# Feed-forward part of a Mamba layer: down projection three tiles behind, gate and up as one row, normalisation spread over engines

## The chip, the cores and the metric

The kernel runs on one core of a Trainium2 chip. Its time is device microseconds of one execution. The hardware profiler also records one execution of the kernel; all durations below are from it.

## The reference

x has 4 x 2048 tokens of 256 channels. Four Mamba layers run on the normalised x, their result is added to x, and a feed-forward part with FP4 rounding follows. Cut to what matters here:

```python
def fp4_quant_dequant(x):          # blocks of 16 along the last dimension
    scale = max(max(abs(block)) / 6.0, 1e-12)
    q = nearest of 0, 0.5, 1, 1.5, 2, 3, 4, 6 to abs(block / scale), with its sign
    return q * scale
def fp4_linear(x, w):
    return fp4_quant_dequant(x) @ fp4_quant_dequant(w).T
def ffn(x, w_gate, w_up, w_down):  # w_gate, w_up: 704 x 256; w_down: 256 x 704
    h = silu(fp4_linear(x, w_gate)) * fp4_linear(x, w_up)
    return fp4_linear(h, w_down)
x = x + mamba_layers(layernorm(x))
x = x + ffn(layernorm(x))
```

## The kernel before

Three parts follow each other, each a block with a program for every engine: `normalise_input`, `mamba_layers` and `fp4_ffn`. The first two are not touched. All data are fp32, and engines meet by semaphores alone: an engine executes its instructions in the order in which the program issues them, and a wait holds all that stands behind it on its engine. So the order within `turn`, written out by hand for each engine, sets everything.

`fp4_ffn` works on 16 chunks `g` of 512 tokens, each of four tiles `t` of 128 tokens (`tau = 4 * g + t` counts the 64 tiles). First the weights are rounded and turned (three pieces of gate and up, two of down). Then, per chunk: GpSimd adds x and the layers' result into `xa` (`add_x2`, L1398), VectorE takes statistics and mean and variance (L1448), ScalarE computes Ln and Exp for the root's first guess, with a table load for them and one more back to the Silu (L1319, L1367), VectorE refines and normalises into `xn` (L1458), and the chunk is rounded with `qa`. Per tile: TensorE turns the tile of `xq` (`turn_x`), ScalarE copies it to `xqT`, TensorE multiplies with the weights (`gate_up`, L1263) into `gate` and `up`, two PSUM banks each, ScalarE takes the Silu into `sg` (L1367), VectorE the product `hid` (L1508), which is rounded with `qh`; TensorE turns the rounded tile `hq` (`go_down`, L1239), ScalarE copies it to `hqT` (three copies, `copy_hT`), TensorE multiplies with `wdT` (`project_down`, L1280) into the one bank `down`, and VectorE adds `x2`, a copy of `xa` (L1363), and writes `res` (L1493), which SyncE stores.

A rounding (class `Fp4`) is a chain over three engines: VectorE takes the blocks' maximum, scale, nudged scale and reciprocal (`scales`, L1061 to L1068), GpSimd divides (L1073), VectorE masks the exponent (L1079), ScalarE turns it into a magic number with a Relu (`magic`, L1085), VectorE adds and takes it off (`shift` L1090, `unshift` L1095), GpSimd multiplies by the scale (L1101). `qh` has two buffers, `qa` one.

In `turn`, while tile `tau` is computed, the rounding of tile `tau - 1` is finished and the down projection of tile `tau - 2` is made; `before(g, t, n)` names the tile n back. The next chunk is added, normalised and rounded beside: statistics and normalisation at t = 0, divide at t = 1, multiply at t = 2. The chunk after that is loaded into `xa` and `xm` at t = 3, once `x2` is kept (t = 2).

## Time and profile before

| | us |
|---|---|
| median of 3 runs | 8876.52 |
| lowest, highest | 8876.08, 8879.55 |
| the profiled execution | 8879.16 |
| its span, first to last instruction | 8877.4 |
| feed-forward part, first gate matmul to the end | 1015.8 |

| engine | busy in the whole span, us |
|---|---|
| TensorE | 6565.6 |
| VectorE | 8002.6 |
| ScalarE | 5352.6 |
| GpSimd | 6905.2 |

The span is cut into 40 slices on the page; the first 35 are the Mamba layers with VectorE near full, the last five the feed-forward part with no engine over half or two thirds. Mean granted TensorE clock is 0.886 of full speed. A share of busy time is a mean over stages; the feed-forward part has to be read from its own timeline.

### The profile page before, as it was taken

To read this page: it belongs to the slowest core of one execution; us is meant where nothing else is said; L and a number is where in the kernel's file an instruction comes from. 1 tells how busy PE (TensorE), PEld (TensorE's weight loads), DVE (VectorE), ACT (ScalarE), POOL (GpSimd) and SP (SyncE) were. 2 spreads that over 40 slices of the span, in tenths; PEclk is the share of its full clock that TensorE was granted. 3 is DMA by queue.
4 is the path that set the end of the run, shared out by engine and by line. 5 is a ranking of instruction groups with operands and counts; after the bars stand their busy time and mean duration, and the time that the engine had idled before them with its cause. 6 is when DMAs were issued, how large, how long until landed. Compare 5 with 4: busy or idle time off the path is not lost. (4 is left out here: it accounts for less than half of the span.)

```text
span 8877.4 us, 97211 instructions
## 1 busy us (share of the span) xinstructions
PE 6565.6 (74%) x21284; PEld 2595.9 (29%) x21284; DVE 8002.6 (90%) x8268; ACT 5352.6 (60%) x8662; POOL 6905.2 (78%) x3198
## 2 busy tenths in 40 slices
PE   3777777778777777777777777777777777646656
PEld 1222222222222222222222222222222222224434
DVE  3999999999999999999999999999999999845555
ACT  2666666666666666666666666666666666422222
POOL 1888888888888888888888889888888889732222
PEclk9899998989899999898899989898989999767888
DMA  4444454544444544454445545444445455310000
GB/s 136 105 105 112 115 119 110 119 122 113 106 110 113 119 111 118 112 128 115 99 113 117 119 110 119 122 113 106 110 113 119 112 117 119 71 36 22 24 26 24
DMA packets 568694, 910.48 MB, mean 103 GB/s; under 512 B 58320, under 2 KB 203088, under 8 KB 566992
## 3 DMA queue, kind: packets, MB, share of 16 engines
q1 hardware_dynamic: 568016, 903.29, 42.4%
q8 instruction: 200, 3.28, 0.2%
q14 instruction: 478, 3.92, 0.2%
HBM read 716.41 MB, written 186.65 MB: 102 GB/s over the span
## 5 line engine op out<-in xcount | busy, mean ns | idle before, releaser
L832 POOL TENSOR_TENSOR hc<-h,crep 128x1024 f32<-128x1024 f32 x2048 | 4785.0, 2361 | 834.8 <-PE acc L473 748.6
L950 DVE TENSOR_TENSOR_SCAN h<-dA,carry,bu 128x512 f32<-128x512 f32 x3072 | 3768.2, 1265 | 92.7 <-ACT dA L603 46.7
L935 DVE TENSOR_TENSOR bu<-durep,B_all 128x1024 f32<-128x1024 f32 x2048 | 2483.2, 1212 | 194.6 <-DMA durep<-du_dram 146.1
L603 ACT ACTIVATE dA<-drep,cur 128x512 f32<-128x512 f32 x4096 | 2618.6, 710 | 14.5 <-DMA drep<-delta_dram 14.5
L455 PE MATMUL B_all<-dtc,spread_b 128*128 128x512 f32 x2048 | 1360.6, 752 | 1638.1 <-DVE bu L935 1636.6
L612 ACT COPY carry<-h 128x4 f32<-128x4 f32 x1023 | 200.9, 196 | 2223.5 <-DVE h L950 2168.7
L473 PE MATMUL acc<-hc,gather 128*32 128x512 f32 x8192 | 1281.8, 702 | 5.5 <-POOL hc L832 5.5
L950 DVE TENSOR_TENSOR_SCAN h<-dA,bu 128x512 f32<-128x512 f32 x1024 | 1196.7, 1206 | 9.9 <-ACT dA L603 7.8
L493 PE MATMUL work<-xT,inw 128*128 128x512 f32 x2048 | 1020.6, 644 | 60.5 <-ACT xT L623 50.0
L455 PEld LDWEIGHTS B_all<-dtc,spread_b 128*128 128x128 f32 x2048 | 367.6, 213 | 2321.5 <-DVE bu L935 2258.2
L503 PE MATMUL work<-xs,taps 128*128 128x512 f32 x2048 | 964.1, 614 | 0.0
L493 PEld LDWEIGHTS work<-xT,inw 128*128 128x128 f32 x2048 | 400.5, 207 | 758.9 <-issue 662.1
L1073 POOL TENSOR_TENSOR f_f_qh_xn<-f_hid,f_f_qh_rec 128x704 f32<-128x704 f32 x64 | 101.5, 1585 | 630.7 <-DVE f_f_qh_rec L1068 630.7
L503 PEld LDWEIGHTS work<-xs,taps 128*128 128x128 f32 x2048 | 376.1, 194 | 617.9 <-issue 617.9
L1280 PE MATMUL f_down<-f_wdT,f_hqT 128*128 128x256 f32 (+1 forms) x768 | 259.7, 494 | 341.1 <-ACT f_hqT L1329 341.1
L531 PE MATMUL work<-outw,sz 128*128 128x256 f32 x2048 | 489.6, 382 | 0.0
L473 PEld LDWEIGHTS acc<-hc,gather 128*32 128x32 f32 x8192 | 173.0, 116 | 979.8 <-issue 688.0
L844 POOL TENSOR_TENSOR quad<-quad,xs 128x2048 f32<-128x2048 f32 x64 | 289.4, 4522 | 160.2 <-ACT quad L701 160.2
L531 PEld LDWEIGHTS work<-outw,sz 128*128 128x128 f32 x2048 | 394.4, 193 | 55.6
L837 POOL TENSOR_TENSOR xc<-xc,quad 128x2048 f32<-128x2048 f32 x64 | 289.9, 4530 | 142.0 <-ACT quad L668 142.0
L462 PE MATMUL acc<-xc,skip 128*128 128x512 f32 x512 | 339.4, 752 | 0.0
L1280 PEld LDWEIGHTS f_down<-f_wdT,f_hqT 128*128 128x128 f32 (+1 forms) x768 | 177.4, 246 | 413.1 <-ACT f_hqT L1329 358.6
(167 smaller groups left out, 7151.8 us busy)
## 6 DMA issues: line engine op xcount, KB each, us to landing
drep<-delta_dram SPq DMA_DIRECT2D x1024, 256.0 KB, 6.0
durep<-du_dram SPq DMA_DIRECT2D x1024, 256.0 KB, 6.7
crep<-c_dram SPq DMA_DIRECT2D x1024, 64.0 KB, 6.5
delta_dram<-za SPq DMA_DIRECT2D x64, 1024.0 KB, 4.3
du_dram<-relu SPq DMA_DIRECT2D x64, 1024.0 KB, 5.3
x_in<-xbuf SPq DMA_DIRECT2D x65, 512.0 KB, 3.8
x_res<-xbuf SPq DMA_DIRECT2D x64, 512.0 KB, 3.9
xbuf<-x_res SPq DMA_DIRECT2D x64, 512.0 KB, 5.6
```

The costliest lines, as they stand in the source:

```text
L455: pe.matmul(B_all[:], spread_b[:, s % QS, :], dtc[:, p_, :], start=True, stop=True).then_inc(bb_ready, 1)
L462: pe.matmul(acc[:], skip[:, q, :], xc[:, p_, q, :], start=True, stop=False, skip_group_check=True)
L473: ins = pe.matmul(acc[32 * k:32 * k + 32, :], gather[:], hc[:, 4 * (s % 2) + k, :], start=False, stop=s % QS == QS - 1, skip_group_check=True)
L493: ins = pe.matmul(W[b][:], inw[:, k, z * DI + e * P:z * DI + (e + 1) * P], xT[:, k, :], start=k == 0, stop=k == KD - 1)
L503: ins = pe.matmul(W[b][:], taps[:, 4 * e + k, :], xs[:, e, k:k + T], start=k == 0, stop=k == 3)
L531: ins = pe.matmul(half, sz[:, p_, k, t * P:(t + 1) * P], outw[:, k, :], start=False, stop=k == DB - 1)
L603: act.activation(dA[:, 4 * (s % 2) + k, :], drep[q % 2][:, k, :], ACT.Exp, scale=cur[:, p_, 4 * s + k:4 * s + k + 1]).then_inc(da_ready, 1)
L832: pool.tensor_tensor(hc[:, pair, :], h[:, pair, :], crep[:, j:j + 1, :].to_broadcast([P, 2, T]), ALU.mult).then_inc(hc_ready, 1)
L837: pool.tensor_tensor(xc[:, p_], xc[:, p_], quad[:], ALU.mult).then_inc(xc_ready, 1)
L935: dve.tensor_tensor(bu[:, 2 * k:2 * k + 2, :], durep[q % 2][:, 2 * k:2 * k + 2, :], B_all[:].unsqueeze(1).to_broadcast([P, 2, T]), ALU.mul ...
L950: dve.tensor_tensor_scan(h[:, r, :], dA[:, r, :], bu[:, k, :], start, ALU.mult, ALU.add).then_inc(scanned, 1)
L1280: ins = pe.matmul(down[:, 0:D], hqT[0:rows, tt % 2, k, :], wdT[0:rows, k, :], start=k == 0, stop=k == GT - 1)
```

## The change

Only `fp4_ffn` and the layout of its weights change; the programs of the Mamba layers have the same instructions in the same order.

- Gate and up weights lie one behind the other without padding between them, and `gate_up` writes one row of 1,408 columns over three banks (`gu`), in pieces of 512, 512 and 384 columns; it waits until the last tile's `hid` is done. `down` has two banks.
- The down projection is three tiles behind, and its transposes stand ahead of the tile's gate/up, its matmuls behind. `hq` has four buffers.
- ScalarE copies `down` to `res` (`copy_res`, four tiles behind), and GpSimd adds `x2` to it (L1476). Two ScalarE copies of the turned tile instead of three.
- Mean and variance come from aggregate instructions on VectorE and small GpSimd operations; the Newton step is on GpSimd, the normalisation itself four ScalarE operations (L1327). Over the next chunk's four tiles: statistics, variance and root at t = 0; normalisation and scales at t = 1; divide, exponent, magic and first rounding at t = 2; second rounding and multiply at t = 3. The chunk after that is added at t = 3 and loaded at t = 1.
- On VectorE a tile's two roundings now stand ahead of the next tile's `hid`.

The diff, cut to its core:

```diff
-        gate, up = ps("gate", [P, 2, T]), ps("up", [P, 2, T])
...
+        gu = ps("gu", [P, 3 * T])
         hT = ps("hT", [P, 2, T])
         xTp = ps("xTp", [P, T])
-        down = ps("down", [P, T])
...
+        down = ps("down", [P, 2, T])
...
-                    at = before(g, t, 2)
-                    if at is not None:
...
-                    if t == 3 and not is_last(g):
+                    if t == 1 and not (isinstance(g, int) and g >= CH - 2):
                         sp.wait_ge(S["x2_kept"], g + 1)
-                        load((g + 2) % CH, par_)
+                        load(g + 2, par_)
+                    if at_least(g, 1):
+                        store(t, NT * g + t - NT)
...
-                for dst, at, sem_, free in ((gate, 0, S["gated"], None), (up, GT * P, S["up_done"], S["hid_ready"])):
...
-                    for half in range(2):
-                        for k in range(KD):
-                            ins = pe.matmul(dst[:, half, 0:HALF], xqT[:, t % 2, k, :],
-                                            wguT[:, k, at + half * HALF:at + (half + 1) * HALF],
-                                            start=k == 0, stop=k == KD - 1)
-                    ins.then_inc(sem_, 1)
+                    pe.wait_ge(S["hid_ready"], tau)
+                for at, width in SEGMENTS:
+                    for k in range(KD):
+                        ins = pe.matmul(gu[:, at:at + width], xqT[:, t % 2, k, :], wguT[:, k, at:at + width],
+                                        start=k == 0, stop=k == KD - 1)
+                    if at + width >= IN and at < IN:
+                        ins.then_inc(S["gated"], 1)
+                ins.then_inc(S["up_done"], 1)
...
                 pe.wait_ge(S["hT_copied"], tau + 1)
...
+                if positive(tau - 1):
+                    pe.wait_ge(S["res_copied"], tau - 1)
...
                     tau = NT * g + t
+                    at = before(g, t, 3)
+                    if at is not None:
+                        go_down(*at)
...
                     gate_up(tau, t)
                     if t < NT - 1:
                         turn_x(t + 1, tau + 1, g, par_)
-                    elif not is_last(g):
+                    if at is not None:
+                        project_down(*at)
+                    if t == NT - 1 and not is_last(g):
                         turn_x(0, tau + 1, g + 1, 1 - par_)
-                    at = before(g, t, 2)
-                    if at is not None:
-                        go_down(*at)
-                        project_down(*at)
...
+            def normalise(n, b):
+                act.wait_ge(S["root_done"], n + 1)
+                act.wait_ge(qa.xn_ready, GP + n)
+                for t in range(NT):
+                    ins = act.activation(xn[:, t], xa[:, b, t], ACT.Identity, bias=shift[:, t:t + 1],
+                                         scale=root[:, t:t + 1])
+                ins.then_inc(S["normed"], 1)
+            def keep_x2(g, b):
+                act.wait_ge(S["x2_ready"], g + 1)
...
+                act.copy(x2[:, b], xa[:, b]).then_inc(S["x2_kept"], 1)
...
+            def copy_res(tt, tau, chunk):
+                act.wait_ge(S["down_done"], tau + 1)
...
+                act.copy(res[:, tt], down[:, tt % 2, 0:D]).then_inc(S["res_copied"], 1)
...
-                    if t == 0 and not is_last(g):
-                        guess_root(g + 1)
-                    if t == 2:
-                        act.wait_ge(S["x2_ready"], g + 1)
...
-                        act.copy(x2[:], xa[:, par_]).then_inc(S["x2_kept"], 1)
+                    if at_least(g, 1):
+                        copy_res(t, tau - NT, g - 1)
+                    at = before(g, t, 3)
+                    if at is not None:
+                        hidden_turned(*at)
+                    at = before(g, t, 1)
+                    if at is not None:
+                        qh.magic(act, DP + at[1], at[0] % 2, minus_magic[:])
+                    if t == 0:
+                        keep_x2(g, par_)
+                    if t == 1 and not is_last(g):
+                        normalise(g + 1, 1 - par_)
                     act.wait_ge(S["gated"], tau + 1)
...
-                    act.activation(sg[:, t % 2].rearrange("p (a b) -> p a b", a=2), gate[:, :, 0:HALF],
-                                   ACT.Silu).then_inc(S["silu_done"], 1)
+                    act.activation(sg[:, t % 2], gu[:, 0:IN], ACT.Silu).then_inc(S["silu_done"], 1)
+                    if t == 0 and not is_last(g):
+                        guess_root(g + 1)
+                    if t == 2 and not is_last(g):
+                        qa.magic(act, GP + g + 1, 0, minus_magic[:])
                     if t < NT - 1 or not is_last(g):
                         copy_xT(t + 1, tau + 1)
-                    at = before(g, t, 1)
-                    if at is not None:
-                        qh.magic(act, DP + at[1], at[0] % 2, minus_magic[:])
...
+            def variance(n):
+                pool.wait_ge(S["means"], n + 1)
+                pool.tensor_tensor(ve[:], mv[:, :, 1], c_eps[:], ALU.add).then_inc(S["var_ready"], 1)
...
+            def newton_step(n):
+                pool.wait_ge(S["guess_ready"], n + 1)
+                pool.tensor_tensor(tmp[:], guess[:], guess[:], ALU.mult).then_inc(S["newton"], 1)
...
+                pool.tensor_tensor(shift[:], minus_mean[:], root[:], ALU.mult).then_inc(S["root_done"], 1)
...
             def turn(g, par_):
                 nxt, other = g + 1, 1 - par_
                 for t in range(NT):
                     tau = NT * g + t
+                    if at_least(g, 1):
+                        pool.wait_ge(S["res_copied"], tau - NT + 1)
+                        if t == 0:
+                            pool.wait_ge(S["x2_kept"], g)
+                        pool.tensor_tensor(res[:, t], res[:, t], x2[:, other, t], ALU.add).then_inc(S["res_ready"], 1)
+                    if not is_last(g):
+                        if t == 2:
+                            qa.divide(pool, GP + nxt, 0, flat_xn)
+                        if t == 3:
+                            quantise_x(nxt, other)
+                    at = before(g, t, 1)
+                    if at is not None:
+                        quantise_h(*at)
                     if t == 0 and not is_last(g):
-                        add_x2(nxt, other)
-                    at = before(g, t, 1)
+                        variance(nxt)
+                    if t == 3 and not (isinstance(g, int) and g >= CH - 2):
+                        add_x2(g + 2, par_)
                     qh.divide(pool, DP + tau, t % 2, hid[:, t % 2])
-                    if t == 1 and not is_last(g):
-                        qa.divide(pool, GP + nxt, 0, flat_xn)
-                    if t == 2 and not is_last(g):
-                        quantise_x(nxt, other)
-                    if at is not None:
...
-                        qh.multiply(pool, DP + at[1], at[0] % 2, hq[:, at[0] % 2])
+                    if t == 0 and not is_last(g):
+                        newton_step(nxt)
...
+            def scales_x(n):
+                dve.wait_ge(S["normed"], n + 1)
+                qa.scales(dve, GP + n, 0, flat_xn)
...
                     at = before(g, t, 1)
-                    if t == 0 and not is_last(g):
-                        normalise(nxt, other, 0)
                     if at is not None:
                         qh.exponent(dve, DP + at[1], at[0] % 2)
...
-                    dve.tensor_tensor(hid[:, t % 2].rearrange("p (a b) -> p a b", a=2),
...
+                    if not is_last(g):
+                        if t == 0:
+                            statistics(nxt, other)
+                        if t == 3:
+                            qa.unshift(dve, GP + nxt, 0)
                     if at is not None:
                         qh.shift(dve, DP + at[1], at[0] % 2)
+                        if t == 0 and not is_last(g):
+                            dve.wait_ge(S["stats"], nxt + 1)
                         qh.unshift(dve, DP + at[1], at[0] % 2)
+                    if not is_last(g):
+                        if t == 0:
+                            if at is None:
+                                dve.wait_ge(S["stats"], nxt + 1)
+                            moments()
+                        if t == 2:
+                            qa.exponent(dve, GP + nxt, 0)
+                    hidden(t, tau)
                     dve.wait_ge(S["hid_ready"], tau + 1)
                     qh.scales(dve, DP + tau, t % 2, hid[:, t % 2])
                     if not is_last(g):
-                        if t == 0:
-                            normalise(nxt, other, 1)
                         if t == 1:
-                            round_x(nxt)
+                            scales_x(nxt)
                         if t == 2:
                             qa.shift(dve, GP + nxt, 0)
-                            qa.unshift(dve, GP + nxt, 0)
-                    at = before(g, t, 2)
-                    if at is not None:
-                        add_residual(at[0], at[1], g if t >= 2 else g - 1)
```

How the instructions stand, in the loop that makes two chunks per iteration. GpSimd, before, one chunk from its first instruction (t = 0 to t = 3; `f_hq` is a tile's multiply, `f_f_qh_xn` its divide, `f_f_qa_xn` and `f_xq` the next chunk's divide and multiply):

```order
L1398 TENSOR_TENSOR f_xa<-f_xa,f_xm 128x1024 [waits f_in_loaded1]
L1073 TENSOR_TENSOR f_f_qh_xn<-f_hid,f_f_qh_rec 128x704 [waits f_qh_rec_ready]
L1101 TENSOR_TENSOR f_hq<-f_f_qh_q,f_f_qh_scale 128x704 [waits f_qh_rounded]
L1073 TENSOR_TENSOR f_f_qh_xn<-f_hid,f_f_qh_rec 128x704 [waits f_qh_rec_ready]
L1073 TENSOR_TENSOR f_f_qa_xn<-f_xn,f_f_qa_rec 128x1024 [waits f_qa_rec_ready]
L1101 TENSOR_TENSOR f_hq<-f_f_qh_q,f_f_qh_scale 128x704 [waits f_qh_rounded,f_hT_ready]
L1073 TENSOR_TENSOR f_f_qh_xn<-f_hid,f_f_qh_rec 128x704 [waits f_qh_rec_ready]
L1101 TENSOR_TENSOR f_xq<-f_f_qa_q,f_f_qa_scale 128x1024 [waits f_qa_rounded]
L1101 TENSOR_TENSOR f_hq<-f_f_qh_q,f_f_qh_scale 128x704 [waits f_qh_rounded,f_hT_ready]
L1073 TENSOR_TENSOR f_f_qh_xn<-f_hid,f_f_qh_rec 128x704 [waits f_qh_rec_ready]
```

The same chunk in the changed kernel, from the third divide on (t = 2 and t = 3):

```order
L1476 TENSOR_TENSOR f_res<-f_res,f_x 128x256 [waits f_res_copied]
L1073 TENSOR_TENSOR f_f_qa_xn<-f_xn,f_f_qa_rec 128x1024 [waits f_qa_rec_ready]
L1101 TENSOR_TENSOR f_hq<-f_f_qh_q,f_f_qh_scale 128x704 [waits f_qh_rounded,f_hT_ready]
L1073 TENSOR_TENSOR f_f_qh_xn<-f_hid,f_f_qh_rec 128x704 [waits f_qh_rec_ready]
L1476 TENSOR_TENSOR f_res<-f_res,f_x 128x256 [waits f_res_copied]
L1101 TENSOR_TENSOR f_xq<-f_f_qa_q,f_f_qa_scale 128x1024 [waits f_qa_rounded]
L1101 TENSOR_TENSOR f_hq<-f_f_qh_q,f_f_qh_scale 128x704 [waits f_qh_rounded,f_hT_ready]
L1417 TENSOR_TENSOR f_xa<-f_xa,f_xm 128x1024 [waits f_in_loaded0]
L1073 TENSOR_TENSOR f_f_qh_xn<-f_hid,f_f_qh_rec 128x704 [waits f_qh_rec_ready]
```

A tile's multiply stood behind its successor's divide and now stands ahead of it; the residual adds are new, and `f_xa` has moved from the chunk's start to behind the last multiply.

VectorE, before, from the product of t = 2 to that of t = 3:

```order
L1068 RECIPROCAL f_f_qh_rec<-f_f_qh_nudged 128x44 [waits f_qh_nudge_done]
L1090 SCALAR_TENSOR_TENSOR f_f_qa_q<-f_f_qa_ex,f_f_qa_xn 128x1024 [waits f_qa_magic_ready]
L1095 SCALAR_TENSOR_TENSOR f_f_qa_q<-f_f_qa_ex,f_f_qa_q 128x1024 [waits f_qa_shifted]
L1493 TENSOR_TENSOR f_res<-f_down,f_x 128x256 [waits f_res_stored0]
L1079 TENSOR_SCALAR f_f_qh_ex<-f_f_qh_xn 128x704 [waits f_qh_xn_ready]
L1508 TENSOR_TENSOR f_hid<-f_sg,f_up 128x704 [waits f_qh_xn_ready,f_up_done,f_silu_done]
L1090 SCALAR_TENSOR_TENSOR f_f_qh_q<-f_f_qh_ex,f_f_qh_xn 128x704 [waits f_qh_magic_ready]
L1095 SCALAR_TENSOR_TENSOR f_f_qh_q<-f_f_qh_ex,f_f_qh_q 128x704 [waits f_qh_shifted]
```

The changed kernel, at the same place:

```order
L1547 TENSOR_TENSOR f_hid<-f_sg,f_gu 128x704 [waits f_qh_xn_ready,f_up_done,f_silu_done]
L1061 TENSOR_REDUCE f_f_qh_amax<-f_hid 128x44 [waits f_qh_done,f_hid_ready]
L1064 TENSOR_SCALAR f_f_qh_scale<-f_f_qh_amax 128x44 [waits f_qh_maxed]
L1066 TENSOR_SCALAR f_f_qh_nudged<-f_f_qh_scale 128x44 [waits f_qh_scaled]
L1068 RECIPROCAL f_f_qh_rec<-f_f_qh_nudged 128x44 [waits f_qh_nudge_done]
L1090 SCALAR_TENSOR_TENSOR f_f_qa_q<-f_f_qa_ex,f_f_qa_xn 128x1024 [waits f_qa_magic_ready]
L1079 TENSOR_SCALAR f_f_qh_ex<-f_f_qh_xn 128x704 [waits f_qh_xn_ready]
L1095 SCALAR_TENSOR_TENSOR f_f_qa_q<-f_f_qa_ex,f_f_qa_q 128x1024 [waits f_qa_shifted]
L1090 SCALAR_TENSOR_TENSOR f_f_qh_q<-f_f_qh_ex,f_f_qh_xn 128x704 [waits f_qh_magic_ready]
L1095 SCALAR_TENSOR_TENSOR f_f_qh_q<-f_f_qh_ex,f_f_qh_q 128x704 [waits f_qh_shifted]
L1547 TENSOR_TENSOR f_hid<-f_sg,f_gu 128x704 [waits f_qh_xn_ready,f_up_done,f_silu_done]
```

The product `f_hid` stood ahead of the last tile's two roundings and is now behind them, the next chunk's first rounding stands at the end of t = 2 and the second between exponent and rounding of t = 3.

ScalarE, before, t = 0 (the chunk's first instructions):

```order
L1319 ACT_TABLE_LOAD
L1321 ACTIVATE f_lnv<-f_ve 128x4 [waits f_var_ready]
L1323 ACTIVATE f_guess<-f_lnv 128x4 [waits f_lnv_done]
L1367 ACT_TABLE_LOAD
L1367 ACTIVATE f_sg<-f_gate 128x704 [waits f_hid_ready]
L1349 COPY f_xqT<-f_xTp 128x256 [waits f_up_done,f_xT_ready]
L1085 ACTIVATE f_f_qh_ex<-f_f_qh_ex,f_minus_magic 128x704 [waits f_qh_ex_ready]
L1326 COPY f_hqT<-f_hT 128x512 [waits f_down_done]
L1328 COPY f_hqT<-f_hT 128x128
L1329 COPY f_hqT<-f_hT 64x128
```

The changed kernel, t = 0:

```order
L1357 COPY f_res<-f_down 128x256 [waits f_res_stored0]
L1338 COPY f_hqT<-f_hT 128x640 [waits f_down_done]
L1339 COPY f_hqT<-f_hT 64x128
L1085 ACTIVATE f_f_qh_ex<-f_f_qh_ex,f_minus_magic 128x704 [waits f_qh_ex_ready]
L1335 COPY f_x<-f_xa 128x1024 [waits f_res_ready]
L1393 ACTIVATE f_sg<-f_gu 128x704 [waits f_hid_ready]
L1316 ACT_TABLE_LOAD
L1318 ACTIVATE f_lnv<-f_ve 128x4 [waits f_var_ready]
L1320 ACTIVATE f_guess<-f_lnv 128x4 [waits f_lnv_done]
L1321 ACT_TABLE_LOAD
L1345 COPY f_xqT<-f_xTp 128x256 [waits f_up_done,f_xT_ready]
```

The two copies of the turned tile stood last and now stand near the front; Ln, Exp and the loads stood ahead of the Silu and are behind it, ahead of the copy to `f_xqT`.

## Rows read from the trace of the kernel before

**Rows 1.** Windows view: stretch, length, busy us of engines, granted clock, DMA share, GB/s.
```profile
8300.40:8365.24 64.84, 40.08 (x145) 26.57 (x144) 35.44 (x62) 15.96 (x30) 18.20 (x12) 0.82 0.07 24
...
7861.60:8877.40 1015.80, 643.14 (x2302) 425.91 (x2302) 557.16 (x966) 251.38 (x474) 282.73 (x173) 0.82 0.07 24
```

**Rows 2.** Timeline, one steady chunk: start, us, engine, line, out<-in [idle before <-releaser].
```profile
8300.40 2.63 PE L1263 MATMUL f_gate<-f_wguT,f_xqT 128*128 128x352 f32 x8
...
8306.85 2.34 POOL L1398 TENSOR_TENSOR f_xa<-f_xa,f_xm 128x1024 f32<-128x1024 f32 x1 [4.94 <-DMA f_xm<-xbuf]
...
8312.01 1.28 ACT L1367 ACT_TABLE_LOAD   x1
...
8337.77 5.65 PE L1280 MATMUL f_down<-f_wdT,f_hqT 128*128 128x256 f32 x12 [11.35 <-ACT f_hqT L1329]
...
8365.24 2.63 PE L1263 MATMUL f_gate<-f_wguT,f_xqT 128*128 128x352 f32 x8
```

**Rows 3.** Timeline, a tile of the last chunk.
```profile
8829.46 2.63 PE L1263 MATMUL f_gate<-f_wguT,f_xqT 128*128 128x352 f32 x8
...
8834.55 0.89 DVE L1508 TENSOR_TENSOR f_hid<-f_sg,f_up 128x704 f32<-128x704 f32 x1 [2.17 <-PE f_up L1263]
...
8836.70 3.05 PE L1280 MATMUL f_down<-f_wdT,f_hqT 128*128 128x256 f32 x12 [1.38 <-ACT f_hqT L1329]
...
8839.69 2.63 PE L1263 MATMUL f_gate<-f_wguT,f_xqT 128*128 128x352 f32 x8
```

**Rows 4.** Timeline, VectorE and GpSimd operations that meet.
```profile
8353.23 1.16 DVE L1090 SCALAR_TENSOR_TENSOR f_f_qa_q<-f_f_qa_ex,f_f_qa_xn 128x1024 f32<-128x1024 f32 x1
...
8353.39 2.24 POOL L1073 TENSOR_TENSOR f_f_qh_xn<-f_hid,f_f_qh_rec 128x704 f32<-128x704 f32 x1 [18.20 <-DVE f_f_qh_rec L1068]
...
8354.42 2.28 DVE L1095 SCALAR_TENSOR_TENSOR f_f_qa_q<-f_f_qa_ex,f_f_qa_q 128x1024 f32<-128x1024 f32 x1
...
8356.78 1.93 POOL L1101 TENSOR_TENSOR f_xq<-f_f_qa_q,f_f_qa_scale 128x1024 f32<-128x1024 f32 x1 [1.16 <-DVE f_f_qa_q L1095]
8356.96 2.14 DVE L1079 TENSOR_SCALAR f_f_qh_ex<-f_f_qh_xn 128x704 uint32<-128x704 uint32 x1
```

**Rows 5.** Timeline of the weights and the first chunk, where roundings run alone.
```profile
7836.02 1.38 POOL L1073 TENSOR_TENSOR f_f_qh_xn<-f_wd_in,f_f_qh_rec 128x704 f32<-128x704 f32 x1 [0.81 <-DVE f_f_qh_rec L1068]
...
7837.44 0.53 DVE L1079 TENSOR_SCALAR f_f_qh_ex<-f_f_qh_xn 128x704 uint32<-128x704 uint32 x1 [1.50 <-POOL f_f_qh_xn L1073]
...
7840.87 1.38 POOL L1101 TENSOR_TENSOR f_wdq<-f_f_qh_q,f_f_qh_scale 128x704 f32<-128x704 f32 x1 [3.47 <-DVE f_f_qh_q L1095]
...
7849.62 1.22 DVE L1061 TENSOR_REDUCE f_f_qa_amax<-f_xn 128x64 f32<-128x1024 f32 x1
...
7851.96 1.93 POOL L1073 TENSOR_TENSOR f_f_qa_xn<-f_xn,f_f_qa_rec 128x1024 f32<-128x1024 f32 x1 [7.40 <-DVE f_f_qa_rec L1068]
...
7868.51 0.89 DVE L1508 TENSOR_TENSOR f_hid<-f_sg,f_up 128x704 f32<-128x704 f32 x1 [3.54 <-PE f_up L1263]
...
7871.30 1.39 POOL L1073 TENSOR_TENSOR f_f_qh_xn<-f_hid,f_f_qh_rec 128x704 f32<-128x704 f32 x1 [8.67 <-DVE f_f_qh_rec L1068]
```

**Rows 6.** Timeline, the last Mamba layer's own normalisation.
```profile
7773.24 1.41 DVE L962 BATCH_NORM_STATS2 stats<-x_res 128x6 f32<-128x256 f32 x4 [21.33 <-ACT x_res L710]
...
7775.14 0.20 POOL L858 TENSOR_TENSOR ve<-mv,c_eps 128x4 f32<-128x4 f32 x1 [21.22 <-DVE mv L967]
...
7777.23 2.07 ACT L721 ACTIVATE x_res<-x_res,shift,root 128x256 f32<-128x256 f32 x4 [1.42 <-POOL shift L873]
```

**Rows 7.** Timeline of TensorE in a Mamba layer.
```profile
5037.42 3.70 PE L503 MATMUL work<-xs,taps 128*128 128x512 f32 x8
5044.41 1.12 PE L455 MATMUL B_all<-dtc,spread_b 128*128 128x512 f32 x2 [3.29 <-DVE bu L935]
...
5046.97 4.84 PE L503 MATMUL work<-xs,taps 128*128 128x512 f32 x8
```

**Rows 8.** Timeline, the last instruction on data.
```profile
8874.66 0.42 DVE L1493 TENSOR_TENSOR f_res<-f_down,f_x 128x256 f32<-128x256 f32 x1 [4.42 <-PE f_down L1280]
```

251 lines of the change are left out of this document (126 added, 125 removed).

## The prediction

> **What bounds the kernel now.** I read the 40 slices first: 35 of them are the four Mamba layers, which the change leaves alone, so only the feed-forward part counts. The windows view gives its length: from the first gate matmul to the end 1015.8 us [rows 1], for 16 chunks of four tiles. Then the timeline of one chunk: its first gate matmul starts at 8300.40 and the next chunk's at 8365.24, a period of 64.84 us, in which TensorE is busy 40.1, VectorE 35.4, GpSimd 18.2 and ScalarE 16.0 us [rows 1, 2]. No engine is full, so waits bound it. The timeline names them. GpSimd's `f_xa` add waits 4.94 us for a transfer issued only at the chunk's end; behind it stand statistics, Ln, a table load and the Silu, and behind that, on ScalarE, the copy of the turned hidden tile that `f_down` waits for. A tile later `f_down` waits 11.35 us for the same copy, which now stands behind the Relu of the next chunk's quantisation, and then takes 5.65 us, in part at the lower of the two clocks (granted 0.5, 1.2 of 2.4 GHz), against 3.05 [rows 2, 3]. In the last chunk, with no next one to prepare, tiles follow every 10.23 us (8829.46 to 8839.69), of which 1.38 is still `f_down` waiting for the copy [rows 3].
>
> **What the changed kernel can reach on TensorE.** Take that wait out: 10.23 - 1.38 = 8.85 us a tile. The gate/up row has the same 2,816 columns in pieces of 512 and 384, not 352. A matmul shows as two records. Eight records of 512 columns take 3.70 us and eight of 352 take 2.63 [rows 3, 7], the last one's tail of some 0.15 in both: 0.44 and 0.31 each, in proportion to their columns. The row costs the same 5 us, with 0.1 for what the tails leave unsure. A tile is then 9.0 us, a chunk 36: the floor. What removes the wait is that the hidden tile is turned before gate/up and its copy, about 1 us of ScalarE, is made during gate/up.
>
> **The rounding chain.** Per tile VectorE and GpSimd hand work to and fro, and the next product `f_hid` now stands behind the last tile's two roundings on VectorE. From rows without contention [rows 5]: product to start of the divide 7871.30 - 7868.51 = 2.79; divide 1.39; divide's end to start of the multiply 7840.87 - (7836.02 + 1.38) = 3.47, in which the exponent is 0.53 and the Relu and the two roundings are near 0.95 each with their handovers; I count 3.35 to the last rounding's end. Alone that is 2.79 + 1.39 + 3.35 = 7.5 us, under TensorE's 9.0. The question is what the chunk's extra work adds.
>
> **The shared port.** At 8353 the divide, 1.38 alone, takes 2.24: it starts 0.16 behind a VectorE rounding of 1.16 and ends 1.38 behind that one's end. The second rounding, of the same size, takes 2.28 and ends 1.07 behind the divide's end. At 8356.96 the exponent, 0.53 alone [rows 5], takes 2.14 and ends after the multiply that started 0.18 before it [rows 4]. So exponents, small scale operations and both roundings on VectorE never overlap a GpSimd tensor operation; who comes first holds the port to its end. After the change the port's work in a chunk is, on VectorE, 4 x (0.53 + 2 x 0.9 + 0.4 for two small ones) + 0.7 + 2 x 1.16 + 0.4 = 14.3 us (0.7: the chunk's exponent, scaled from 704 columns to 1,024), and on GpSimd 8 x 1.38 + 2 x 1.93 + 2.34 (the `f_xa` add) + eight small ones at 0.2 [rows 6] to 0.28 (1.8) + four residual adds: 21.5. No row shows a 256-column add: a quarter of the 1,024-column `f_xa` add is 0.59, and I take 0.6 (0.4, what VectorE needs for it, to 0.9). That is 35.8 us of a 36 us chunk: the port cannot be fully packed, so it and not TensorE decides.
> The Trainium skill ("Perfetto Trace Analysis", Optimizing Scalar/DVE Operations) says that moving work between GpSimd and VectorE may not help because they share a port. That speaks against the residual adds and the Newton steps on GpSimd; by it they are a part of the sum, as below.
>
> **One steady chunk, walked in order.** I count from the end of one tile's divide to the end of the next one's, with the program orders shown for the change. Where both engines want the port, the earlier one gets it; VectorE's next instruction starts some 0.1 us before GpSimd sees its semaphore.
> - Tile 0: residual add 0.6 (the exponent waits for it) + exponent 0.53 + statistics 1.4 (they cover the Relu; with the aggregate 1.9 [rows 6]) + roundings 1.85 + aggregate 0.4 + product to divide 2.7 + divide 1.39 = 8.9, less 0.2 where one instruction starts before the last one's end: 8.7.
> - Tile 1: five Newton operations 1.3 (they and the residual add let exponent and roundings through only in gaps); the normalisation, now four ScalarE operations, 2.07 by the same lines in the layer [rows 6], stands before the Silu, so the product starts 4.8 after the divide's end. + 2.8, then the scales of the next chunk, 2.34 by 7851.96 - 7849.62 [rows 5], which collide with the divide (1.4, beside them) and the add: +0.5. Until the chunk's scales are ready: 10.4.
> - Tile 2: exponent 0.45, the chunk's divide 1.93, and only then the roundings 1.85, the chunk's exponent 0.7, product to scales 2.7, the chunk's first rounding ahead of the divide 1.1, divide 1.38 = 10.1.
> - Tile 3: residual add 0.6, exponent 0.55, the chunk's second rounding 1.15, rounding 0.9, the chunk's multiply 1.93 (it was queued before the second rounding), rounding 0.9, product and maximum 1.7; then the `f_xa` add of 2.34, queued behind this tile's multiply, holds the port, +2.1 before the scales 0.85, divide 1.4 = 12.1.
> Sum 41.3 us; I take 41.2, since neighbours overlap by 0.1. TensorE needs 36 of it, so it idles 5.2. Most of that lies in one place: gate/up of tile 1 waits for the copy of its input, which stands on ScalarE behind Ln, Exp and a table load of 1.28 [rows 2], and these behind the variance, which GpSimd does after a multiply. `f_down` and the transposes before it are done 4.2 us earlier.
> **The clock.** Shortly after an idle stretch of 3.29 us the convolution's matmuls took 4.84 us, where they take 3.70 [rows 7]: 1.1 lost in this group alone; `f_down` after 11.35 us lost 2.6 [rows 2, 3]. I take 1.7, between them. The wait of 4.2 us is longer than the first, and the gate/up behind it has no slack there (its end starts the product), so all of it counts. A steady chunk is then **42.9 us**.
> **Off the path.** The longer residual path (ScalarE copy, GpSimd add, four tiles later), the `x2` copy (1.0, before a Silu with slack), one copy of 640 columns for two, stores and the loads, issued half a chunk earlier (the 4.94 us wait goes): 0. ScalarE has under 22 us of work. If the copies were late they would cost `f_down` up to 1.4 a tile, as now.
>
> **The whole.** Before the first gate/up: normalisation of chunk 0 by GpSimd and ScalarE instead of VectorE, about +1.1 (bounds 0 and 2). Chunk 0, without earlier tiles to finish, but with the cold clock: 37. Chunks 1 to 14: 14 x 42.9 = 600.6. Last chunk: its first gate/up starts 5.3 before the preceding divide ends; then 4 regular tiles to the last product, 28.4, and from there 0.9 + 1.9 + 1.4 + 3.35 + 1.4 + transposes 0.9, copy 1.0, `f_down` 3 to 5, copy and add 1.0, and 2.3 as now from the last residual's end (8875.08) to the end [rows 8]: 52.4 in all. Together 690 + 1.1 = 691 against 1015.8: **-324.7**. The span 8877.4 becomes 8552.7; the profiled execution took 8879.16, 1.8 more than its span, and 2.6 more than the median, so 8877 - 325 = **8552 us**.
>
> **Rivals.**
> - *The idle wait does not lower the clock*: chunk 41.2, 24 us less: 8528. For it: the fall shows some way behind the idle stretch, so part of it may find the engine waiting anyway.
> - *TensorE is the bound*, the port's collisions being hidden: chunk 36.5, 90 us less: 8463. For it: the last tiles of before run at 8.85 without the wait, though with VectorE at 6.1 of 10.2 [rows 1, 3]. Against: rows 4.
> - *GpSimd wins the ties*: the chunk's divide ahead of the exponent (+1.0), its multiply ahead of a rounding (+1.0), a tile's multiply ahead of the chunk's exponent (+0.7), and later variance (+0.4): chunk 46, 8596. The outer bound, VectorE's 31 and GpSimd's 21.5 never overlapping, is 52.5: 8688.
> - *Slower than before*: TensorE at its lower clock throughout. Every tile then costs 9.0 x 2 less its 0.4 of fixed parts = 17.6, a chunk 70.5, 5.6 more than now, x 14: 8955. It decides from 16.2 a tile, that is when over 80% of the time is at the lower clock. Against: a mean of 0.82 now [rows 1], with gaps of 10 us; mine are of 4.
> - *It does not do what it says*: the next chunk's input late again. The load is issued about 25 us ahead of its add, which waited 4.94: chance below 0.01.
>
> **Chances.** Forecast 0.51, no fall of the clock 0.15, TensorE bound 0.14, lost ties 0.17, TensorE at its lower clock 0.03, of which 0.01 lands within 0.2% of before because only most of the tiles are slow. Range 8465 to 8612: the forecast with residual adds of 0.4 to 0.9 (4 x 14 x 0.25 = 14 us), no fall, most of the third and of the fourth case. Faster by over 0.2% (18 us, about what a measurement of this kernel tells from no change): 0.97; within: 0.01; slower 0.02.
>
> **What would show it.** Right: chunks of 42 to 44 us; exponents in tile 2 or scales in tile 3 of 2 us behind GpSimd's operations; one idle stretch of TensorE of about 4 us before the second gate/up, for the copy of `f_xqT`, with the granted clock at 0.5 behind it. Wrong: uniform tiles of 9 us with TensorE near 100% (second rival), or TensorE waiting for `f_hid` in most tiles (more ties lost). If GpSimd's adds and VectorE's roundings are seen side by side at their own durations, the sum fails at the port.

## The result: 8522.8 us, 29 us below the forecast, and the profile after

| | before | after |
|---|---|---|
| median | 8876.3 us | 8522.8 us (8518.0 to 8525.1) |
| profiled execution and its span | 8879.16, 8877.4 | 8524.19, 8522.4 |
| a steady chunk | 64.84 | 40.97 |
| first gate matmul, start | 7861.6 | 7860.75 |

The ratio is 0.9604 (95% interval 0.9587 to 0.9621). All medians in this document are of executions in the chip's fast state; one of the four of e9 below took 8910.2 us at a lower clock and is left out. The Mamba layers are untouched; the feed-forward part went from 1015.8 us [rows 1] to 661.65. The windows view of the changed kernel, with the columns of rows 1 (a steady chunk, then the whole part):

```profile
8197.58:8238.55 40.97, 36.11 (x128) 21.34 (x128) 31.73 (x47) 19.43 (x35) 23.48 (x24) 0.96 0.12 38
7860.75:8522.40 661.65, 582.42 (x2046) 342.07 (x2046) 494.18 (x737) 304.75 (x534) 365.58 (x357) 0.95 0.11 35
```

TensorE is busy for 36.1 of 41.0 us, VectorE 31.7, GpSimd 23.5, and the mean granted clock rose from 0.82 to 0.96. The 4.94 us that GpSimd waited for the transfer and the 11.35 us that `f_down` waited for its copy [rows 2] have no counterpart in the steady chunk. One long wait of TensorE is left. The timeline of the second tile shows it (start, us, engine, line, out<-in, idle before and its releaser):

```profile
8193.83 1.39 POOL L1101 TENSOR_TENSOR f_hq<-f_f_qh_q,f_f_qh_scale 128x704 f32<-128x704 f32 x1 [3.56 <-DVE f_f_qh_q L1095]
...
8195.17 0.20 POOL L1421 TENSOR_TENSOR f_ve<-f_mv,f_c_eps 128x4 f32<-128x4 f32 x1
...
8195.41 0.20 ACT L1318 ACTIVATE f_lnv<-f_ve 128x4 f32<-128x4 f32 x1 [0.95 <-POOL f_ve L1421]
...
8195.87 1.28 ACT L1321 ACT_TABLE_LOAD   x1
...
8197.16 0.37 ACT L1345 COPY f_xqT<-f_xTp 128x256 f32<-128x256 f32 x1
...
8197.58 6.42 PE L1258 MATMUL f_gu<-f_wguT,f_xqT 128*128 128x512 f32 x12 [4.31 <-ACT f_xqT L1345]
...
8202.75 0.76 ACT L1393 ACTIVATE f_sg<-f_gu 128x704 f32<-128x704 f32 x1 [1.01 <-PE f_gu L1258]
...
8204.10 0.89 DVE L1547 TENSOR_TENSOR f_hid<-f_sg,f_gu 128x704 f32<-128x704 f32 x1 [2.20 <-PE f_gu L1258]
```

The chain is to be read downwards: GpSimd's multiply, behind it the variance, then Ln on ScalarE, the table load, the copy to `f_xqT`, and only then gate/up, after 4.31 us of idle. Gate/up takes 6.42 us, where the other tiles take 4.89 to 4.96, and the Silu and the product wait for it (2.20). The granted clock, microsecond by microsecond (the column behind the engines' busy times):

```profile
8196.00:8197.00 1.00, 0.00 (x0) 0.00 (x0) 0.60 (x2) 1.00 (x1) 0.28 (x1) 1.00 1.07 359
8197.00:8198.00 1.00, 0.41 (x1) 0.42 (x2) 0.00 (x0) 0.99 (x4) 1.00 (x1) 0.55 0.06 17
8198.00:8199.00 1.00, 1.00 (x2) 0.42 (x2) 0.53 (x1) 0.85 (x3) 0.84 (x4) 0.50 0.00 0
8199.00:8200.00 1.00, 1.00 (x2) 0.34 (x1) 0.39 (x1) 0.92 (x2) 0.85 (x3) 0.50 0.00 0
8200.00:8201.00 1.00, 1.00 (x3) 0.45 (x2) 0.97 (x1) 1.00 (x3) 0.23 (x1) 0.75 0.00 0
8201.00:8202.00 1.00, 1.00 (x4) 0.41 (x3) 0.89 (x1) 0.74 (x2) 0.00 (x0) 1.00 0.39 131
```

It stands at 0.50 (1.2 of 2.4 GHz) from 8198 to 8200 and is back at 1.00 from 8201 on: some 3 us at half speed, which is the 1.5 us that this gate/up takes more than the others. And the port that VectorE and GpSimd share, at five places of a chunk (the first in the chunk before):

```profile
8189.54 0.72 POOL L1476 TENSOR_TENSOR f_res<-f_res,f_x 128x256 f32<-128x256 f32 x1
8189.61 1.03 DVE L1079 TENSOR_SCALAR f_f_qh_ex<-f_f_qh_xn 128x704 uint32<-128x704 uint32 x1 [1.50 <-POOL f_f_qh_xn L1073]
...
8206.73 1.16 DVE L1061 TENSOR_REDUCE f_f_qa_amax<-f_xn 128x64 f32<-128x1024 f32 x1
8206.89 1.39 POOL L1073 TENSOR_TENSOR f_f_qh_xn<-f_hid,f_f_qh_rec 128x704 f32<-128x704 f32 x1 [3.46 <-DVE f_f_qh_rec L1068]
...
8208.24 0.72 POOL L1476 TENSOR_TENSOR f_res<-f_res,f_x 128x256 f32<-128x256 f32 x1
8208.36 0.65 DVE L1066 TENSOR_SCALAR f_f_qa_nudged<-f_f_qa_scale 128x64 f32<-128x64 f32 x1
...
8221.26 2.51 POOL L1101 TENSOR_TENSOR f_xq<-f_f_qa_q,f_f_qa_scale 128x1024 f32<-128x1024 f32 x1 [1.60 <-DVE f_f_qa_q L1095]
8222.02 2.50 DVE L1095 SCALAR_TENSOR_TENSOR f_f_qh_q<-f_f_qh_ex,f_f_qh_q 128x704 f32<-128x704 f32 x1
...
8226.01 2.35 POOL L1417 TENSOR_TENSOR f_xa<-f_xa,f_xm 128x1024 f32<-128x1024 f32 x1
8226.28 2.12 DVE L1064 TENSOR_SCALAR f_f_qh_scale<-f_f_qh_amax 128x44 f32<-128x44 f32 x1
```

The exponent (0.53 alone [rows 5]) takes 1.03 behind the residual add, a scale step of 64 columns 0.65 (0.20 in e11 below, where no add stands beside it), the rounding 2.50 behind `f_xq` (0.89 alone), a scale of 44 columns 2.12 behind the `f_xa` add. The pair at 8206.73 is the counterexample: a reduction and a divide side by side, each at its own duration. The Trainium skill ("SBUF — State Buffer", section "SBUF: two separate sides") has the pair of ports as an exclusive lock, which a VectorE operation needs in a two-port mode or with two SBUF inputs, and which whoever starts first holds for the whole instruction. The roundings, with two inputs in SBUF, were held, and the reduction, with one input, was not; that agrees. The exponent and the scale steps also have one input and were held, so by that sentence they must run in a two-port mode, which no view here shows.

### The profile page after: what moved, and what is told of

It is laid out like the page before. It is cut to its first block and busy times, and to the rows that moved or that the text cites. A ratio compares the mean times of both kernels' runs of the same rounds, so it can differ in the third digit from the quotient of the medians.

```text
span 8522.4 us, 96647 instructions
## 1 busy us (share of the span) xinstructions
PE 6497.0 (76%) x21028; PEld 2513.0 (29%) x21028; DVE 7936.9 (93%) x8028; ACT 5407.2 (63%) x8725; POOL 6990.0 (82%) x3390
## 5 line engine op out<-in xcount | busy, mean ns | idle before, releaser
L1258 PE MATMUL f_gu<-f_wguT,f_xqT 128*128 128x512 f32 (+1 forms) x768 | 341.7, 598 | 72.8 <-ACT f_xqT L1345 65.9
L854 POOL TENSOR_TENSOR relu<-za,xc 128x2048 f32<-128x2048 f32 x64 | 290.5, 4539 | 0.1
L850 POOL TENSOR_TENSOR za<-quad,relu 128x2048 f32<-128x2048 f32 x64 | 290.0, 4531 | 0.1
```

Of the source, the lines that this page charges most:

```text
L854: pool.tensor_tensor(relu[:], za[:], xc[:, p_], ALU.mult).then_inc(du_ready, 1)
L1258: ins = pe.matmul(gu[:, at:at + width], xqT[:, t % 2, k, :], wguT[:, k, at:at + width], start=k == 0, stop=k == KD - 1)
```

## Experiments

The experiments were run in three groups, each on a chip of its own beside the kernel before, whose median there was 8876.4 us (e1 to e4), 8872.3 (e6 to e9) and 8870.0 (e10, e11, b1, b3). So a difference of medians between two groups is uncertain by some 6 us, and the ratio or the chunk is the safer measure. A chunk's length is the distance of one gate/up from the same one of the next chunk.

| kernel | median us | ratio to before, 95% | chunk us |
|---|---|---|---|
| changed kernel | 8522.8 | 0.9587 to 0.9621 | 41.0 |
| e1 copy first | 8501.9 | 0.9563 to 0.9595 | 39.2 |
| e2 idle filled | 8532.1 | 0.9597 to 0.9629 | 41.0 |
| e3 add early | 8497.2 | 0.9556 to 0.9588 | 39.1 (mean) |
| e4 thin residual | 8519.0 | 0.9582 to 0.9614 | 41.0 |
| e8 = e4 and e1 | 8478.6 | 0.9537 to 0.9569 | 37.7 |
| e7 = e1 and e3 | 8487.5 | 0.9549 to 0.9581 | 38.7 |
| e9 turned behind | 8517.5 | 0.9584 to 0.9623 | 40.3 |
| e6 product first | 8633.2 | 0.9712 to 0.9745 | 47.8 |
| e10 = e6 and e1 | 8575.9 | 0.9651 to 0.9683 | 44.4 |
| e11 residual on VectorE, with e1 | 8470.8 | 0.9531 to 0.9563 | 37.8 |
| b1, before with Relu behind the copy | 8732.2 | 0.9827 to 0.9860 | 54.6 |
| b3 = b1 and load ahead | 8684.3 | 0.9774 to 0.9807 | 51.2 |

### The idle wait and the clock: e1, e2

e1 puts the copy to `f_xqT` ahead of Ln, Exp and the table load, on ScalarE:

```diff
                     act.activation(sg[:, t % 2], gu[:, 0:IN], ACT.Silu).then_inc(S["silu_done"], 1)
-                    if t == 0 and not is_last(g):
-                        guess_root(g + 1)
                     if t == 2 and not is_last(g):
                         qa.magic(act, GP + g + 1, 0, minus_magic[:])
                     if t < NT - 1 or not is_last(g):
                         copy_xT(t + 1, tau + 1)
+                    if t == 0 and not is_last(g):
+                        guess_root(g + 1)
```

> One move in the changed kernel: at t = 0 ScalarE copies the next tile's input to f_xqT ahead of Ln, Exp and their two table loads, not behind them. Theory (chain over VectorE and GpSimd through the shared port, plus a clock fall after the idle stretch): gate/up of t = 1 starts at the end of the last product, 2.7 us earlier, at full clock, and takes 4.9 instead of 6.4 us; the product of t = 1 is then held by the normalisation, the Silu and the roundings and comes 1.55 us earlier. Chunk 40.96 -> 39.4 us, time 8523 -> about 8500. If TensorE's work were the bound: the whole idle stretch of 4.3 us is won, chunk 36.7, about 8459. If GpSimd and VectorE alone set the period and the clock costs nothing: 8523 unchanged.

It measured 8501.9 us, as expected. The wait of 4.31 us is gone, and that gate/up takes 4.96 us. But the clock still falls in about every second chunk, at another gate/up, the one behind the Relu of the next chunk's rounding. Timeline of e1, two chunks in a row:

```profile
8204.82 6.62 PE L1258 MATMUL f_gu<-f_wguT,f_xqT 128*128 128x512 f32 x12 [1.58 <-ACT f_xqT L1345]
...
8244.00 4.99 PE L1258 MATMUL f_gu<-f_wguT,f_xqT 128*128 128x512 f32 x12 [1.49 <-ACT f_xqT L1345]
```

The chunks with and without this fall are 39.2 and 39.3 us long, so here the lower clock costs nothing: the next product does not wait for this group's end. e2 leaves the wait and fills it with matmuls whose results nobody uses:

```diff
                         go_down(*at)
+                    if t == 1 and at is not None:
+                        pe.wait_ge(S["res_copied"], tau - 4)
+                        for _ in range(14):
+                            pe.matmul(down[:, at[0] % 2, D:2 * D], ident[:], wdT[:, 0, :], start=True, stop=True)
                     gate_up(tau, t)
```

> Added in the changed kernel: at t = 1 TensorE executes 14 matmuls of 256 columns into an unused half bank, 3.5 us, in the stretch in which it waits for f_xqT; their results are not used. Nothing waits less. Theory of the clock fall: gate/up of t = 1 starts as before but takes 4.9 instead of 6.4 us, chunk 40.96 -> 39.5, about 8502. If the idle stretch had nothing to do with the long gate/up, or if TensorE were the bound: unchanged at 8523 or slower by up to what the filler overruns, 0.5 us a chunk, 8530.

It measured 8532.1 us, a miss. The timeline of TensorE and ScalarE in e2, then the window of its gate/up:

```profile
8194.74 6.21 PE L1302 MATMUL f_down<-f_wdT,f_ident 128*128 128x256 f32 x28
...
8198.78 0.37 ACT L1349 COPY f_xqT<-f_xTp 128x256 f32<-128x256 f32 x1
...
8200.78 4.89 PE L1258 MATMUL f_gu<-f_wguT,f_xqT 128*128 128x512 f32 x12
```

```profile
8200.78:8205.67 4.89, 4.89 (x15) 2.39 (x14) 2.26 (x2) 3.25 (x6) 2.38 (x4) 1.00 0.08 27
```

Gate/up takes 4.89 us at a granted clock of 1.00. So it is the idle stretch that brings the low clock to this group. But I had counted the 14 matmuls as 14 records, and a matmul is two: the filler took 6.21 us instead of 3.5 and ended 1.6 us after the copy (8198.78 + 0.37 to 8200.78). That is as much as the clock had cost (1.5), hence the same chunk of 41.0. The mechanism is shown, the gain of a better-sized filler is not.

### The port: e4, e8, e11

e4 cuts GpSimd's residual add to one column; its output lacks `x2` in the other 255.

```diff
-                        pool.tensor_tensor(res[:, t], res[:, t], x2[:, other, t], ALU.add).then_inc(S["res_ready"], 1)
+                        pool.tensor_tensor(res[:, t, 0:1], res[:, t, 0:1], x2[:, other, t, 0:1], ALU.add).then_inc(S["res_ready"], 1)
```

> The residual adds in GpSimd's loop are made for one of 256 columns (the output lacks x2 elsewhere): 0.72 us each becomes about 0.15. Shared port theory: the exponents of t = 0 and t = 3 (1.03 instead of 0.53), a rounding of t = 1 (1.36 instead of 0.89) and a small operation of t = 2 (0.65 instead of 0.19) no longer wait, about 1.8 us a chunk: 39.2, about 8497. Without a shared port: GpSimd has idle time ahead of each of its other operations, so nothing, 8523.

It measured 8519.0 us, no gain clear of the noise, though the port theory asked for 26 us. The timeline of e4 has both halves of the answer:

```profile
8188.63 7.89 PE L1258 MATMUL f_gu<-f_wguT,f_xqT 128*128 128x512 f32 x12 [3.58 <-ACT f_xqT L1345]
...
8190.65 0.89 DVE L1090 SCALAR_TENSOR_TENSOR f_f_qh_q<-f_f_qh_ex,f_f_qh_xn 128x704 f32<-128x704 f32 x1 [0.95 <-ACT f_f_qh_ex L1085]
...
8196.61 0.89 DVE L1547 TENSOR_TENSOR f_hid<-f_sg,f_gu 128x704 f32<-128x704 f32 x1 [4.14 <-PE f_gu L1258]
```

The rounding behind the add is back at its own 0.89 (1.36 in the changed kernel), so the port is relieved. But gate/up of the same tile now takes 7.89 instead of 6.42 us and the product waits 4.14 for it: this time the lower clock (0.63 in the mean over this group) covered more of it, 3.0 us more than 4.89 against 1.5, and it took the gain back. The wait ahead of it is shorter than in the changed kernel, 3.58 us against 4.31, so the deeper fall does not come from a longer idle stretch, as I wrote in the expectation of e8. e8 tests that reading by making the same cut with the copy first (the same part of the output is missing):

> The residual add cut to one column (the output lacks x2 in the other 255), together with the copy to f_xqT ahead of Ln and Exp. The thin add alone gave 8519, no gain, though the VectorE steps behind it went back to their own durations. My theory: the gain was eaten by the longer idle of TensorE and the deeper fall of its clock ahead of the second gate/up of a chunk; with the copy first that wait is gone, and the port time comes through: 8502 less 15 x 1.8 = 8475. Rival: the residual adds' port time was hidden all along: 8500.

It measured 8478.6 us, 23 us under e1 (1.5 a chunk), where 27 were expected and the rival had none. Its chunk:

```profile
8191.64:8229.36 37.72, 34.95 (x128) 20.76 (x128) 29.79 (x48) 18.85 (x35) 21.34 (x23) 1.00 0.13 42
```

A clock of 1.00 throughout and 37.7 us. The residual adds do cost what they hold of the port. GpSimd's own time is not what they cost: in e1 it waits 0.7 to 3.6 us behind each of the four adds for its next input. e11 turns that into a kernel with the whole output: VectorE adds `x2` straight from PSUM, in gaps in which it waits, and the ScalarE copy and the GpSimd add go.

```diff
+            def add_residual(t, tau, g_of, b):
+                dve.wait_ge(S["down_done"], tau + 1)
...
+                dve.tensor_tensor(res[:, t], down[:, t % 2, 0:D], x2[:, b, t], ALU.add).then_inc(S["res_ready"], 1)
...
                         qh.exponent(dve, DP + at[1], at[0] % 2)
+                    if t in (1, 2) and at_least(g, 1):
+                        add_residual(t, tau - NT, g - 1, other)
...
                             qa.shift(dve, GP + nxt, 0)
+                    if t in (0, 3) and at_least(g, 1):
+                        add_residual(t, tau - NT, g - 1, other)
```

> The changed kernel with the early copy to f_xqT, and with the residual add on VectorE straight from PSUM, as in before (0.42 there), in the gap in which VectorE waits for the Relu (t = 1, 2) or for the divide (t = 0, 3); no ScalarE copy to f_res, no GpSimd add. Port theory: the 0.72 us of GpSimd leave the port in every tile, and the 0.42 on VectorE fall into gaps: as with the one-column add, chunks of 37.8, 8479. Rival (VectorE's own time counts, and its read of x2 holds the port too): 39.3 + 4 x 0.4, 8520.

It measured 8470.8 us, 52 us under the changed kernel and the fastest kernel with the whole output (e8 lies within its interval). Timeline and window of e11:

```profile
8215.60 2.08 POOL L1073 TENSOR_TENSOR f_f_qa_xn<-f_xn,f_f_qa_rec 128x1024 f32<-128x1024 f32 x1 [0.94 <-DVE f_f_qa_rec L1068]
8215.82 0.41 DVE L1522 TENSOR_TENSOR f_res<-f_down,f_x 128x256 f32<-128x256 f32 x1
```

```profile
8221.46:8259.27 37.81, 35.17 (x129) 20.72 (x129) 31.01 (x52) 17.68 (x31) 20.74 (x19) 1.00 0.12 42
```

The add runs beside GpSimd's divide and still takes 0.41, as in before (0.42 [rows 8]): with one input in PSUM it does not need the port. The Trainium skill ("Perfetto Trace Analysis", Optimizing Scalar/DVE Operations) says that moving work between the two engines might not help, since they share a read port. Here it helped, by 31 us against e1 (28 by the two ratios), because the operation left the port altogether. The ScalarE copy that e11 also saves adds little, as e8 keeps it and has the same chunk. TensorE is now busy for 35.2 of 37.8 us, so little is left above its floor of 36.

### The long add: e3, e7

e3 moves the `f_xa` add from t = 3 to t = 1:

```diff
-                    if t == 3 and not (isinstance(g, int) and g >= CH - 2):
+                    if t == 1 and not (isinstance(g, int) and g >= CH - 2):
                         add_x2(g + 2, par_)
```

> One move in the changed kernel: GpSimd's 1,024-column f_xa add stands at t = 1, behind the tile's multiply, where GpSimd has 3.4 us without work and VectorE makes the product and the maximum, not at t = 3, where a small scale operation of VectorE takes 2.12 instead of 0.19 us behind it. The same work on every engine. Shared port theory: 1.9 us less a chunk, 39.05, about 8496. If the sum of GpSimd's work, or TensorE, sets the period: 8523, unchanged. If the loads come too late for the earlier place (issued 11 us ahead of it): slower, by what the add waits.

It measured 8497.2 us, as expected. e7 makes both edits:

> Both edits at once: the copy to f_xqT ahead of Ln and Exp, and the f_xa add at t = 1 instead of t = 3. Alone they gave 8501.9 and 8497.2 against 8522.8. Chain theory: the two touch different tiles (the copy tile 1, the add tile 3), so the savings add up: 1.4 + 1.7 us a chunk, chunks of 37.8, 8476. TensorE theory: with 9.0 us a tile TensorE is at 36 of these 37.8, so the second saving partly runs into it: chunks of 38.5, 8487.

It measured 8487.5 us, the second figure, but not for its reason. Timeline of e3 at the add, in one chunk and (the last line) in the next, then of e7:

```profile
8189.16 2.36 POOL L1417 TENSOR_TENSOR f_xa<-f_xa,f_xm 128x1024 f32<-128x1024 f32 x1
...
8189.97 0.89 DVE L1547 TENSOR_TENSOR f_hid<-f_sg,f_gu 128x704 f32<-128x704 f32 x1 [2.29 <-PE f_gu L1258]
...
8191.81 0.19 DVE L1064 TENSOR_SCALAR f_f_qh_scale<-f_f_qh_amax 128x44 f32<-128x44 f32 x1
...
8229.41 1.28 DVE L1064 TENSOR_SCALAR f_f_qh_scale<-f_f_qh_amax 128x44 f32<-128x44 f32 x1
```

```profile
8181.01 2.35 POOL L1417 TENSOR_TENSOR f_xa<-f_xa,f_xm 128x1024 f32<-128x1024 f32 x1
...
8181.87 1.53 DVE L1064 TENSOR_SCALAR f_f_qh_scale<-f_f_qh_amax 128x44 f32<-128x44 f32 x1
```

In e3's first chunk the add begins while VectorE waits 2.29 us for a gate/up that ran partly at the lower clock (6.51 us), and the scale behind the product takes 0.19. In the next chunk the same gate/up ran at full clock (4.99), the wait is 0.76, and the scale takes 1.28. In e7 the wait is gone altogether and the scale takes 1.53. So an earlier product only waits longer for the end of the add: e3's second chunk is 38.7 us long, as those of e7 are, and the early copy gains only where e3's clock had fallen (39.1 to 39.3). It was the late gate/up of tile 1 that gave the add its free port. TensorE is not the reason: in e7 it still idles 2.5 to 2.9 us ahead of one gate/up, in another tile, and the chunk is 38.7 whether that gate/up takes 4.99 us or 6.6. So two gains of 21 and 26 us made 35.

### Turning ahead of gate/up: e9

The change's most visible step is to turn `f_hq` ahead of gate/up, so that the copy is made meanwhile. e9 takes it back:

```diff
-                    if at is not None:
-                        go_down(*at)
                     gate_up(tau, t)
                     if t < NT - 1:
                         turn_x(t + 1, tau + 1, g, par_)
                     if at is not None:
+                        go_down(*at)
                         project_down(*at)
```

On ScalarE the two copies move from the tile's start to behind the Silu.

> The transposes of f_hq moved behind gate/up, the two copies to f_hqT behind the Silu: f_down waits for the copy again, as in before (1.38 us there), everything else as in the changed kernel. Chain theory: TensorE needs 9.0 + 1.4 = 10.4 us a tile against 10.2 of the chain; tiles 1 and 3 have slack, tiles 0 and 2 (8.6 and 9.4) do not: +1 to +3 us a chunk, 8538 to 8568. If TensorE were the bound already: +1.4 a tile, 8524 + 61 x 1.4 = 8609. Nothing or a gain: the waits stand elsewhere.

It measured 8517.5 us, with the changed kernel's ratio of 0.9604: neither +1 to +3 a chunk nor +1.4 a tile, but the last case, "nothing or a gain". Timeline and window of e9:

```profile
8186.77 4.99 PE L1258 MATMUL f_gu<-f_wguT,f_xqT 128*128 128x512 f32 x12 [0.32 <-ACT f_xqT L1344]
...
8193.58 3.05 PE L1276 MATMUL f_down<-f_wdT,f_hqT 128*128 128x256 f32 x12 [0.94 <-ACT f_hqT L1338]
```

```profile
8186.77:8227.11 40.34, 35.67 (x128) 20.84 (x128) 31.96 (x48) 19.45 (x35) 23.34 (x24) 1.00 0.12 39
```

`f_down` waits 0.94 us for the copy again. But TensorE's work now lies later, and the gate/up that waited 4.31 us waits 0.32 and takes 4.99. The idle time of a chunk is much the same, 40.34 - 35.67 = 4.7 us against 40.97 - 36.11 = 4.9; in pieces of about 1 us it left the clock at 1.00 in this kernel, with one piece of 4.3 in the changed one it did not. As I read it, the clock gave back what the late copies cost; e9 does not price the two apart.

### The product behind the roundings: e6, e10

e6 puts `f_hid` ahead of the last tile's roundings again, on VectorE:

```diff
+                    hidden(t, tau)
                     if at is not None:
                         qh.shift(dve, DP + at[1], at[0] % 2)
...
                             qa.exponent(dve, GP + nxt, 0)
-                    hidden(t, tau)
```

> VectorE's product f_hid ahead of the last tile's two roundings, as in before, instead of behind them. Chain theory: the product covers the Relu (0.95), so a tile's chain is 0.7 shorter where gate/up is done in time; gate/up ends only 0.3 us before the last divide's end, so in about half of the tiles the product waits for the Silu with the roundings behind it: -1.5 us a chunk, 8501, with bounds of 8480 and 8540. Rival: the wait for the Silu now delays the roundings of every tile by 1 us or more: 8570.

It measured 8633.2 us: my forecast of 8501 has the wrong sign, and the rival (8570) is too small. Timeline of e6:

```profile
8159.27 8.02 PE L1258 MATMUL f_gu<-f_wguT,f_xqT 128*128 128x512 f32 x12 [6.22 <-ACT f_xqT L1345]
...
8167.38 0.89 DVE L1547 TENSOR_TENSOR f_hid<-f_sg,f_gu 128x704 f32<-128x704 f32 x1 [7.74 <-PE f_gu L1258]
...
8168.19 0.88 DVE L1090 SCALAR_TENSOR_TENSOR f_f_qh_q<-f_f_qh_ex,f_f_qh_xn 128x704 f32<-128x704 f32 x1
```

The product waits 7.74 us for gate/up, and the last tile's roundings, whose Relu was done 6 us earlier, are queued behind it. I had priced the distance between gate/up and the product per tile, and missed that it closes a loop: gate/up, product, roundings, multiply, variance, table load, copy, next gate/up, 15.0 us for that tile (13.1 in the changed kernel). The clock adds to it, with 8.02 us for 4.9 here and 6.69 in a second group of each chunk, behind a wait of 2.10. e10 opens that loop with the early copy:

> The changed kernel with f_hid ahead of the roundings (8633 alone, chunks of 47.8) and with the copy to f_xqT ahead of Ln and Exp (8502 alone). Theory: f_hid first costs because it closes a loop in one tile: product, roundings, multiply, variance, table load, copy, gate/up, Silu, next product, with TensorE idle for 6.2 us and slow for 3.1. The early copy opens it: 47.8 - 6 = 42, 8545. Rival: each tile loses by itself (the product waits for the Silu and the roundings stand behind it): 46, 8605.

It measured 8575.9 us, midway between the two. Timeline of e10:

```profile
8240.41 7.26 PE L1258 MATMUL f_gu<-f_wguT,f_xqT 128*128 128x512 f32 x12 [4.54 <-ACT f_xqT L1345]
```

The wait has moved two tiles on, to a copy to `f_xqT` that stands behind the Relu of the chunk's quantisation: 4.54 us idle, and gate/up takes 7.26. The other half I put down to the product's own wait in each tile: in e10 it is 1.2 to 3.8 us in all four, in e1 0.5 at most, and e10 is still 74 us above e1. Having the product behind the roundings is thus worth 110 us of the change as it stands.

### Where before lost its time: b1, b3

b1 is the kernel before with one edit on ScalarE:

```diff
-                    if t == 1 and not is_last(g):
-                        qa.magic(act, GP + g + 1, 0, minus_magic[:])
                     at = before(g, t, 2)
...
                         copy_hT(hqT[:, at[0] % 2]).then_inc(S["hT_copied"], 1)
+                    if t == 1 and not is_last(g):
+                        qa.magic(act, GP + g + 1, 0, minus_magic[:])
```

> The kernel before with one edit on ScalarE: at t = 1 the Relu of the next chunk's quantisation behind the copies to f_hqT instead of ahead. This wait is 11.35 us of a chunk in before, with a slow f_down behind it. If the removed waits carry the gain: a tile of 22.8 us falls to about 12, 15 x -10 = -150, 8726. Rival (the wait is only cover for the slow rounding chain behind it): under 50 us, 8830 or more.

It measured 8732.2 us, where 8726 were expected. b3 adds SyncE's load ahead of the store:

```diff
+                    if t == 3 and not is_last(g):
+                        sp.wait_ge(S["x2_kept"], g + 1)
+                        load((g + 2) % CH, par_)
                     at = before(g, t, 2)
...
                         sp.dma_start(ov[tau], res[:, tt]).then_inc(res_stored[tt], 16)
-                    if t == 3 and not is_last(g):
...
-                        sp.wait_ge(S["x2_kept"], g + 1)
-                        load((g + 2) % CH, par_)
```

> The same, and on SyncE at t = 3 the load ahead of the store, so that the f_xa add of the next chunk no longer waits 4.94 us for its transfer. Removed waits theory: another 5 us a chunk, 8726 - 75 = 8650, so that two moved lines give two thirds of the change's 354 us. Rival: the store isn't what delays the load, or the Ln, table load and Silu behind the add set the tile anyway: nothing beyond the first edit.

It measured 8684.3 us, where 8650 were expected. Timeline of b1 (the transfer's wait and the two longest waits of `f_down`), then of b3:

```profile
8211.91 4.48 PE L1280 MATMUL f_down<-f_wdT,f_hqT 128*128 128x256 f32 x12 [3.75 <-ACT f_hqT L1329]
...
8232.94 2.34 POOL L1398 TENSOR_TENSOR f_xa<-f_xa,f_xm 128x1024 f32<-128x1024 f32 x1 [3.84 <-DMA f_xm<-xbuf]
...
8242.03 4.79 PE L1280 MATMUL f_down<-f_wdT,f_hqT 128*128 128x256 f32 x12 [9.58 <-ACT f_hqT L1329]
```

```profile
8209.63 2.35 POOL L1396 TENSOR_TENSOR f_xa<-f_xa,f_xm 128x1024 f32<-128x1024 f32 x1
...
8218.72 5.07 PE L1278 MATMUL f_down<-f_wdT,f_hqT 128*128 128x256 f32 x12 [5.71 <-ACT f_hqT L1327]
```

The wait of 11.35 us is 3.75 in b1, and the chunk 10.2 us shorter. In b3 the `f_xa` add no longer waits for the transfer, but the chunk gains 3.4 of the 5 us that I expected: the `f_down` behind Ln, table load, Silu and copy still waits 5.71 and then takes 5.07, so the clock again takes a part. Of the 23.9 us by which the change shortens a chunk, these two moves alone give 13.6, a good half and not the two thirds that I expected. The other 10.2 belong to what stays different between b3 and the changed kernel: the Silu behind the table load, the product's place and the tiles between. Only the product is priced by a run (6.8 in e6, from the other side), the rest is not.

## The prediction, step by step

The forecast of 8552 was 29 us high (0.3%), and the time lies in the range.

- **The waits that go** (late transfer, Relu ahead of the copy): right; b1 shows the second by itself, at 10.2 us a chunk, and b3 the first on top of it, at 3.4.
- **TensorE's floor of 36 us**: right. Gate/up measures 4.89 to 4.96 us (5 taken). That TensorE is not the bound is right too: e3 shortens the chunk by a move on GpSimd alone, and e8 by 1.5 us against e1 by a thinner GpSimd add.
- **The port**: right, with every collision that the walk named (the rows of after above). The ties went as walked: the exponent of tile 2 started at 8209.52, 0.16 ahead of the chunk's divide, and kept its 0.46. The residual add measured 0.72, not 0.6, inside its bounds.
- **The walk**, from a tile's divide to the next, with the end of the chunk's scales as the border between tiles 1 and 2: 8.5, 11.5, 9.4 and 11.6 us (8.7, 12.1 with the clock, 10.1 and 12.1 predicted). Here is the error: 42.9 against 41.0, or 28.5 of the 30 us between predicted and measured span. The sign "chunks of 42 to 44 us" failed with it. The term that was mis-sized is the "less 0.2 where one instruction starts before the last one's end": I took it once, in tile 0, and 0.1 for all neighbours together. An instruction of VectorE that doesn't need the one before starts some 0.1 us before that one's record ends, and one that the port held back is held for less than its neighbour's full time. Tile 2 is the plainest: 9.4 for 10.1, and each of its seven terms was 0.03 to 0.2 too long. The rows of before already had the second half: the prediction says that the divide at 8353.39 ended 1.38 behind the rounding's end, but [rows 4] give 8355.63 - 8354.39 = 1.24. Three rows of tile 2:

```profile
8212.55 0.89 DVE L1095 SCALAR_TENSOR_TENSOR f_f_qh_q<-f_f_qh_ex,f_f_qh_q 128x704 f32<-128x704 f32 x1
...
8213.36 0.69 DVE L1079 TENSOR_SCALAR f_f_qa_ex<-f_f_qa_xn 128x1024 uint32<-128x1024 uint32 x1
...
8213.96 0.88 DVE L1547 TENSOR_TENSOR f_hid<-f_sg,f_gu 128x704 f32<-128x704 f32 x1
```

  The rounding ends at 8213.44 and the exponent has started at 8213.36; that one ends at 8214.05 and the product has started at 8213.96.
- **The clock**: right in place, releaser (`f_xqT`, 4.31 us idle against 4.2) and size (1.5 against 1.7). e2 shows that the idle stretch is its cause, e4 that the loss is on the path. That the fall was 1.5 us and not 3.0, as in e4, the prediction had no means to tell; its 1.7 was a choice between two rows. The rival without a fall gave 8528 (chunks of 41.2), nearer to the result than the forecast, and is nonetheless refuted: in it the missing fall (1.5 a chunk) and the walk's excess (1.7) would have cancelled.
- **"What removes the wait is that the hidden tile is turned before gate/up"**: true of the wait, not of the time. e9 puts a wait of about 1 us back and the time stays. The section "off the path" priced late copies at up to 1.4 us a tile; with them the chunk became 0.6 us shorter. The prediction did not ask what an evenly spread wait does to the clock.
- **The product behind the roundings** was in the walk as a cost of 0.95 a tile for the Relu, and its benefit nowhere. e6 shows it to be the largest single step of those that I took back, 110 us.
- **The ends**: first gate/up at 7860.75 (7862.7 predicted), first chunk 38.4 us (37), last 51.1 (52.4). Together -1.8, with the steady chunks' -28.5 the whole difference of -30.3.
- **Rivals**: TensorE bound and lost ties are refuted by the chunk's length and by the rows; TensorE slow throughout by the clock of 0.96; the late load by a `f_xa` add that starts at 8226.01, right behind the multiply.

## What to carry to other kernels

When an edit that relieves a resource gives nothing (e4), look at what the time freed has become before the theory is dropped: here a matmul group behind an idle stretch ran longer at the lower clock and took it; the same edit without that wait gave 23 us. On an engine that works in program order, an instruction that waits for a long producer (the product behind gate/up) belongs behind the work that is ready, and a copy that releases TensorE ahead of anything that waits for another engine. Gains of two edits need not add up: one may have used a wait that the other removes (e3 and e7).

## What the runs showed of the hardware

- A wait's length alone does not tell whether TensorE's clock falls, nor how far. In e3 the same gate/up behind 2.38 us of idle took 4.99 us in one chunk and 6.69 in another; in e1 6.62 behind 1.58 us and 4.99 behind 1.49; in e4 a wait of 3.58 us cost 3.0 us, in the changed kernel one of 4.31 cost 1.5; in e11 waits of 0.2 to 1.2 us ahead of three of every four gate/ups left the clock at 1.00. What decides between them was not found.
- A VectorE addition with one input in PSUM and one in SBUF ran in 0.41 us beside a GpSimd divide (e11), while the roundings with two SBUF inputs did not run beside one, and even a scale of 44 columns, 0.19 us alone, took up to 2.3 beside a GpSimd add of 1,024 columns (e6).
- A GpSimd addition of 256 columns took 0.72 us, over a quarter of the 2.35 for 1,024, which leaves some 0.2 us of fixed cost; the one-column add of e4 took 0.19.
